# VectorE takes two low parts of the second attention earlier, and one of them from GpSimd

## The chip, the core and the metric

The program runs on one core of one Trainium2 chip. The metric is the device time of one execution in microseconds (us); lower is better. The engines of the core are named as the profile names them: PE is TensorE's matmul (PEld its weight loads), DVE is VectorE, ACT is ScalarE, POOL is GpSimd, SP is SyncE, which here only issues DMAs. Each engine runs its own list of instructions in the order in which it was written, and waits on semaphores for the others.

## What is computed

Two transformer layers on 4 batches of 512 tokens of width 256. The first layer is a softmax attention and a linear layer, the second a lightning attention with 16 heads of width 128 and a mixture of 8 experts. In each layer both halves stand between a normalisation with a modulation per batch and a gated addition to the residual `x`:

```python
h = _layernorm(x, axis=-1) * (1 + ca) + sa
x = x + ga * _L0_attn_ref(h, ...)
h = _layernorm(x, axis=-1) * (1 + cb) + sb
x = x + gb * _L0_ffn_ref(h, ...)
...
h = _layernorm(x, axis=-1) * (1 + ca) + sa
x = x + ga * _L1_attn_ref(h, ...)     # the second attention
h = _layernorm(x, axis=-1) * (1 + cb) + sb
x = x + gb * _L1_ffn_ref(h, ...)
```

The second attention, cut to what it multiplies (silu is applied to q, k and v, and the decays depend on the head):

```python
qkv = jax.nn.silu(jnp.einsum('bnf,of->bno', x, w_qkv))
o_inter = jnp.einsum('bhmd,bhde->bhme', qi * q_decay, kv)
qk = jnp.einsum('bhmd,bhnd->bhmn', qi, ki) * diag_decay
o_intra = jnp.einsum('bhmn,bhne->bhme', qk, vi)
out = norm_w * (out * jax.lax.rsqrt(var + EPS))
gate = jax.nn.sigmoid(jnp.einsum('bnf,of->bno', x, w_gate))
return jnp.einsum('bno,fo->bnf', gate * out, w_out)
```

## The kernel before

The work is written by hand as one list per engine. Before the second attention stands the front stage (the first layer), behind it the experts stage. `attention1_stage` is the second attention. It runs over 8 pairs of heads (`PAIRS`), and within a pair over 8 units (`UNITS`): a unit is one batch and one head of the pair, 512 tokens. `attention1_order` gives PE's order within a unit `u`: four blocks of scores `("s", u, 0..3)`, the projections `k` and `q` of the next unit, two projections `v` (or the output product `y`), the projection `g` of the gate, and the four products `pv` of the unit before. Scores and projections share a ring of four PSUM banks; PE waits for a bank until the engine that reads it is through (`emptied`).

**High and low parts.** Products in single precision are made of three products of fp32r parts. ACT copies a tensor into its high part, and a subtraction (whole minus high) makes the low part: `low` in DVE's list, line 1727, or `lower` of `LastPost`, line 372. PE can take a tensor only when its low part is there. `silu_split` on ACT makes the silu of q or k (line 1619) and its high part (line 1622), and `qk_low(which, unit, it)` on DVE the low part, where `which` is 1 for k and 0 for q. The first unit's k and q carry the number -1, and are projected before the second attention begins. `masked` (line 1746) is DVE's product of a block of scores in PSUM and the decay mask; `scores_hi` (line 1647) and `scores_low` (line 1727, tile `attn_pp`) split it. The scores of unit 0 wait for `qk_low(1, -1, 0)` and `qk_low(0, -1, 0)` (`k_ready`, `q_ready`).

**The first layer's last batch.** The front stage leaves the last of the four batches unfinished; `LastPost` ends it inside the first pair of the second attention, spread over the units:

- `tensor_at`, `scalar_aot`, `tensor_out` (lines 264, 271, 278 and 280): the attention's output product, ahead of everything else of the stage.
- `vector_attended` (lines 286 and 295) gates it and adds it to `x`; `vector_stats` (lines 317 and 320) takes mean and variance; `pool_rstd` (lines 327 to 334) takes the reciprocal root.
- `scalar_norm` (line 341), on ACT at the end of unit 0, normalises; `tensor_turn` (line 350), on PE in unit 1 ahead of `("s", 1, 1)`, transposes; `scalar_ht` (lines 362 and 367), on ACT in unit 1, modulates and makes the high part; `lower` (line 372) the low part, before the change on POOL.
- `tensor_ff` (line 380), on PE ahead of `("k", 2)`, is the linear layer, 24 matmuls. It waits for `low_done`, which `lower` raises. A second round of norm, turn, `scalar_ht` and `lower` follows in units 3 and 4 for the second attention's own input of that batch; its `lower` is on DVE already.

POOL also makes the low parts of the first pair's weights, in three parts (line 1873: 1280, 512 and 256 columns), and sums squares (line 1883). SP clears the table of expert rows in DRAM and loads the next pair's weights.

Of the kernel before, what the change touches and what calls it, by code (L numbers as in the profile page):

```python
# [1304 lines left out]
def attention1_stage(nc, t, d):  # L1305
# [14 lines left out]
    with ExitStack() as ctx:  # L1320
# [26 lines left out]
        post = LastPost(n, t, ps, Y_BANK, late_norm.ht)  # L1347
# [60 lines left out]
        with nc.Block() as block:  # L1408
# [316 lines left out]
            def _(dve):  # L1725
# [55 lines left out]
                dve.wait_ge(norm_loaded, 16)  # L1781
                nc.vector.tensor_scalar(normw[:, :], normw[:, :], 0.5, None, ALU.mult).then_inc(norm_halved, 1)
                dve.wait_ge(norm_halved, 1)
                post.vector_attended(nc, dve)
                post.vector_stats(nc, dve, 0)
                qk_low(1, -1, 0)
                qk_low(0, -1, 0)

                def body(it, first, last_pair):
                    for u in range(UNITS):  # L1790
                        more = not (last_pair and u == UNITS - 1)
                        if u == 2:

                            dve.wait_ge(wo_loaded, it * 16 + 16)
                            for h in range(2):
                                nc.vector.tensor_scalar(woraw[:, h, :], woraw[:, h, :], normw[:, at(it * 2 + h)], None,
                                                        ALU.mult).then_inc(wo_scaled, 1)
                        if late(it, u, 2):
                            gate_unit(u - 2, it)
                        masked(u, 0, it)  # L1800
                        if late(it, u, 2):
                            y_low(u - 2, it)
                        if first and u == 3:
                            post.vector_stats(nc, dve, 1)
                        scores_low(u, 0, it)
                        masked(u, 1, it)
                        if more:
                            qk_low(1, u, it)
                        scores_low(u, 1, it)
                        if u == UNITS - 2 and not last_pair:  # L1810
                            weights_low(0, it + 1)
                        if u == UNITS - 1 and not last_pair:
                            weights_low(1, it + 1)
                        if u == 0 and not first:
                            weights_low(2, it)
                        masked(u, 2, it)
                        if first and u == 2:
                            post.vector_fed(nc, dve)
                        if last_pair and u == NORM_AT:
                            late_norm.vector_mean(nc, dve, 0, 0, Y_BANK)  # L1820
                        if last_pair and u == NEXT_AT:
                            late_norm.vector_mean(nc, dve, 1, 1, Y_BANK)
                        if last_pair and u == TURN_AT - 1:
                            late_norm.vector_stats(nc, dve, 0, 0)
                        if last_pair and u == TURN_AT:
                            late_norm.vector_norm(nc, dve, 0, 0)
                        if more:
                            qk_low(0, u, it)
                        scores_low(u, 2, it)
                        if first and u == 4:  # L1830
                            post.lower(dve, nc.vector, 1)
                        masked(u, 3, it)
                        if u % 2 == 0:
                            values_low(0, u, it)
                        elif late(it, u, 3):
                            if not first and u == 1:
                                dve.wait_ge(zeroed, 1)
                            if last_pair and u == UNITS - 1:
                                gate_unit(u - 1, it)
                            else:  # L1840
                                add_output(u, 0, it, first)
                        scores_low(u, 3, it)
                        if u % 2 == 0:
                            values_low(1, u, it)
                        elif late(it, u, 3) and not (last_pair and u == UNITS - 1):
                            add_output(u, 1, it, first)
# [15 lines left out]
            @block.gpsimd  # L1862
            def _(pool):
                nc.gpsimd.memset(t["ones1"][:, :], 1.0).then_inc(ones_set, 1)
                nc.gpsimd.memset(empty[:, 0:D], 0.0).then_inc(empty_set, 1)
                nc.gpsimd.memset(empty[:, D:D + 2], -1.0).then_inc(empty_set, 1)
                nc.gpsimd.memset(empty[:, D + 2:D + 4], 0.0).then_inc(empty_set, 1)
                nc.gpsimd.iota(no_token[:, :], [[P, E * B * TB]], base=2 * B * S, channel_multiplier=1,
                               allow_small_or_imprecise_dtypes=True).then_inc(empty_set, 1)

                def weights_low(part, it):
                    pool.wait_ge(w_hi[part], it + 1)
                    nc.gpsimd.tensor_tensor(wp[:, 1, :, PART[part]], wraw[:, :, PART[part]],
                                            wp[:, 0, :, PART[part]].bitcast(F32), ALU.subtract).then_inc(w_ready[part], 1)

                def sum_unit(u, it):

                    b, h = (u % UNITS) // 2, u % 2
                    pool.wait_ge(squared, it * UNITS + (u + 1))
                    if h == 1:  # L1880
                        pool.wait_ge(summed, it * UNITS + u)
                    cols = ssq[:, b * S:(b + 1) * S]
                    nc.gpsimd.tensor_tensor(cols, cols, sq[:, h, :], ALU.add).then_inc(summed, 1)  # L1883

                sums_zeroed = n.sem("sums_zeroed")
                for b in (0, 2):
                    nc.gpsimd.memset(ssq[:, b * S:(b + 1) * S], 0.0).then_inc(sums_zeroed, 1)
                for part in (1, 0, 2):
                    weights_low(part, 0)
                post.pool_rstd(nc, pool, 0)  # L1890

                def body(it, first, last_pair):
                    for u in range(UNITS):
                        if first and u == 1:
                            nc.gpsimd.memset(yacc[:, NT - TB:NT, :], 0.0).then_inc(zeroed, 1)
                            nc.gpsimd.memset(ssq[:, S:2 * S], 0.0).then_inc(sums_zeroed, 1)
                            post.pool_biased(nc, pool)
                            post.lower(pool, nc.gpsimd, 0)
                        if first and u == 3:
                            post.pool_rstd(nc, pool, 1)  # L1900
                            nc.gpsimd.memset(ssq[:, 3 * S:4 * S], 0.0).then_inc(sums_zeroed, 1)
                            pool.wait_ge(sums_zeroed, 4)
                        if late(it, u, 2):
                            if first and u == 2:
                                pool.wait_ge(sums_zeroed, 3)
                            sum_unit(u - 2, it)
                        if first and u == 2:
                            post.pool_fed(nc, pool)
                        if u == 2:
                            pool.wait_ge(wo_hi, it + 1)  # L1910
                            nc.gpsimd.tensor_tensor(wop[:, 1], woraw[:, :, :], wop[:, 0].bitcast(F32),
                                                    ALU.subtract).then_inc(wo_ready, 1)
                        if last_pair and u == NORM_AT:
                            late_norm.pool_rms(nc, pool, 0, 0)
                            late_norm.pool_update(nc, pool, 0, 0)
                        if last_pair and u == TURN_AT - 1:
                            late_norm.pool_rstd(nc, pool, 0)
                        if last_pair and u == NEXT_AT:
                            late_norm.pool_rms(nc, pool, 1, 1)
                        if last_pair and u == NEXT_AT + 1:  # L1920
                            late_norm.pool_update(nc, pool, 1, 1)

                over_pairs(pool, body)
                for u in (UNITS - 2, UNITS - 1):
                    sum_unit(u, PAIRS - 1)
                late_norm.pool_rstd(nc, pool, 1)
# [1092 lines left out]
```

## Time and profile before

| | us |
|---|---|
| median of three runs | 1178.83 |
| lowest, highest | 1176.25, 1179.16 |
| the profiled execution | 1185.24 |
| its span, first to last instruction | 1183.4 |
| PE busy in it | 1069.6 (90%) |
| DVE busy | 918.9 (78%) |
| ACT busy | 734.4 (62%) |
| POOL busy | 337.7 (29%) |
| mean granted TensorE clock | 0.953 of full |

The second attention begins in the trace 262 us after the span's start and ends at about 975 us. From 330 to 975 us PE is busy for 641.78 of 645 us. Times in the rows below count from the span's start. A row of the timeline gives an instruction's start and how long it took, or the first start and the whole time of several merged ones. Two instructions of one engine may overlap by about 0.1 us, since an engine starts one that doesn't depend on the one before while that drains. A wait names the engine whose signal came last.

### The profile page before, as it was taken

What the parts mean: (1) busy time and instruction counts of PE and PEld (TensorE: products, weight loads), DVE (VectorE), ACT (ScalarE), POOL (GpSimd) and SP (SyncE); (2) the same over time, 40 slices, a digit from 0 to 9 for tenths busy, and PEclk for the clock granted to TensorE, in tenths of its full rate; (3) what the DMA queues carried; (4) which work ended last, traced back from release to release, by engine and by line L of the source; (5) the groups of instructions that cost most, each with busy time, mean ns of one, the idle gap of its engine ahead of it and who ended that gap; (6) DMA issues with size and microseconds to landing.
All of it is one profiled execution on the core that took longest, in us unless ns stands there. A gap on an engine that the chain in (4) does not pass through costs nothing. (4 is left out here: it accounts for less than half of the span.)

```text
span 1183.4 us, 21636 instructions
## 1 busy us (share of the span) xinstructions
PE 1069.6 (90%) x7268; PEld 917.4 (78%) x7268; DVE 918.9 (78%) x1859; ACT 734.4 (62%) x1390; POOL 337.7 (29%) x347
## 2 busy tenths in 40 slices
PE   6879787777999999999999999999999997769994
PEld 5645555556888998899889988998999886659992
DVE  6688888846778878788778778788788788777775
ACT  5668686766567566666666666666666654625650
POOL 3375454443311111101111111111111244743440
PEclk9989898978999999999999999999999998879997
DMA  7210000109504004004004003004001000453436
GB/s 276 71 45 10 15 6 15 41 22 81 118 1 126 10 2 125 9 9 116 9 9 116 9 9 116 9 9 116 9 13 33 1 1 27 141 175 100 127 91 222
DMA packets 62326, 72.16 MB, mean 61 GB/s; under 512 B 21842, under 2 KB 49618, under 8 KB 61235
## 3 DMA queue, kind: packets, MB, share of 16 engines
q1 hardware_dynamic: 58850, 61.90, 19.9%
q0 software_dynamic: 3408, 9.39, 2.1%
q8 instruction: 39, 0.64, 0.2%
q14 instruction: 29, 0.23, 0.1%
HBM read 36.39 MB, written 32.78 MB: 58 GB/s over the span
## 5 line engine op out<-in xcount | busy, mean ns | idle before, releaser
L1475 PE MATMUL all_psum<-all_h_parts,attn_wp 128*128 128x512 f32 x1140 | 296.7, 396 | 0.0
L1647 ACT CAST attn_pp<-attn_p 128x512 fp32r<-128x512 f32 (+3 forms) x256 | 117.4, 458 | 200.8 <-DVE attn_p L1746 198.7
L1475 PEld LDWEIGHTS all_psum<-all_h_parts,attn_wp 128*128 128x128 f32 x1140 | 209.4, 189 | 39.6
L1883 POOL TENSOR_TENSOR all_gate<-all_gate,attn_sq 128x512 f32<-128x512 f32 x64 | 84.8, 1325 | 496.3 <-ACT attn_sq L1658 496.2
L1727 DVE TENSOR_TENSOR attn_pp<-attn_p,attn_pp 128x512 fp32r<-128x512 f32 (+3 forms) x256 | 200.1, 782 | 8.6 <-ACT attn_pp L1647 8.6
L1554 PE MATMUL all_psum<-attn_qkp 128*128 128x512 f32 (+3 forms) x768 | 164.6, 323 | 7.7 <-DVE attn_qkp L1727 7.7
L1501 PE MATMUL all_psum<-attn_pp,attn_vp 128*128 128x512 f32 (+3 forms) x768 | 163.2, 321 | 1.1 <-DVE attn_pp L1727 0.6
L1501 PEld LDWEIGHTS all_psum<-attn_pp,attn_vp 128*128 128x128 f32 x768 | 128.9, 189 | 21.6 <-issue 1.4
L1554 PEld LDWEIGHTS all_psum<-attn_qkp 128*128 128x128 f32 x768 | 124.4, 190 | 16.4 <-DVE attn_qkp L1727 6.2
L1746 DVE TENSOR_TENSOR attn_p<-all_psum,attn_mask 128x512 f32<-128x512 f32 (+3 forms) x256 | 123.7, 483 | 6.6 <-PE all_psum L1554 5.4
L1003 DVE TENSOR_REDUCE front_top<-all_psum 128x2 f32<-128x256 f32 (+3 forms) x128 | 100.8, 816 | 26.5 <-PE all_psum L650 26.2
L1727 DVE TENSOR_TENSOR attn_yp<-attn_y,attn_yp 128x512 fp32r<-128x512 f32 x64 | 45.6, 713 | 77.2 <-ACT attn_yp L1655 77.2
L803 ACT ACTIVATE front_probs<-all_psum 128x1024 f16<-128x1024 f32 (+3 forms) x128 | 83.4, 707 | 33.8 <-PE all_psum L657 33.7
L1470 PE MATMUL all_psum<-attn_wp,all_h_parts 128*128 128x256 f32 x768 | 100.6, 280 | 0.0
L1485 PE MATMUL all_psum<-all_wop,attn_yp 128*128 128x256 f32 x744 | 96.5, 278 | 0.8 <-DVE attn_yp L1727 0.8
L1727 DVE TENSOR_TENSOR attn_qkp<-attn_qk,attn_qkp 128x512 fp32r<-128x512 f32 x128 | 88.1, 689 | 10.2 <-ACT attn_qkp L1622 10.2
L1470 PEld LDWEIGHTS all_psum<-attn_wp,all_h_parts 128*128 128x128 f32 x768 | 94.6, 188 | 0.0
L1485 PEld LDWEIGHTS all_psum<-all_wop,attn_yp 128*128 128x128 f32 x744 | 91.0, 188 | 1.0 <-DVE attn_yp L1727 1.0
L1622 ACT CAST attn_qkp<-attn_qk 128x512 fp32r<-128x512 f32 x128 | 79.5, 621 | 4.1
L1619 ACT ACTIVATE attn_qk<-all_psum 128x512 f32<-128x512 f32 x128 | 75.7, 592 | 3.4 <-PE all_psum L1475 3.3
L657 PE MATMUL all_psum<-front_qt,front_kt 128*128 128x512 f16 (+3 forms) x256 | 56.5, 333 | 19.2 <-ACT front_probs L803 8.7
L1727 DVE TENSOR_TENSOR attn_vp<-attn_v,attn_vp 128x512 fp32r<-128x512 f32 x64 | 44.3, 692 | 32.1 <-ACT attn_vp L1640 32.1
(375 smaller groups left out, 1844.6 us busy)
## 6 DMA issues: line engine op xcount, KB each, us to landing
expert_rows<-attn_empty SPq DMA_DIRECT2D x8, 2080.0 KB, 11.3
all_wraw<-in_w1p SPq DMA_DIRECT2D x8, 1024.0 KB, 5.9
all_yacc<-expert_rows SPq DMA_DIRECT2D x39, 130.5 KB
attn_mask<-decay_masks SPq DMA_DIRECT2D x16, 256.0 KB, 2.7
experts_wx<-expert_results SPq DMA_DIRECT2D x6, 512.0 KB, 8.3
experts_xraw<-in_wx SPq DMA_DIRECT2D x4, 608.0 KB
all_wraw<-in_wx SPq DMA_DIRECT2D x4, 608.0 KB
all_x<-in_x SPq DMA_DIRECT2D x4, 512.0 KB, 7.3
```

Source lines behind the costliest of these rows:

```text
L803: nc.scalar.activation(probs[:, pr, j, :, 0:S - j * P], banks(ev)[:, :, 0:S - j * P], ACT.Exp, scale=D0 ** -0.5).then_inc(exp_done, 1)
L1003: nc.vector.tensor_reduce(top[:, tt, h:h + 2], banks(ev)[:, :, 0:(tt + 1) * P], AX.X, ALU.max).then_inc(top_done, 1)
L1470: last = nc.tensor.matmul(out[:, i * 2 * P:(i + 1) * 2 * P], hh[:, a, k, tt * P:(tt + 1) * P], wp[:, c, k, col:col + 2 * P], start=(m == 0 ...
L1475: last = nc.tensor.matmul(out, wp[:, a, k, col:col + P], hh[:, c, k, b * S:(b + 1) * S], start=(m == 0), stop=(m == 5))
L1485: last = nc.tensor.matmul(ps[:, Y_BANK + i, half * D:(half + 1) * D], yp[:, a, h, tt * P:(tt + 1) * P], wop[:, c, h, :], start=(m == 0), s ...
L1501: last = nc.tensor.matmul(ps[:, O_BANK + h, j * P:S], vp[:, b % 2, a, j, h * P:(h + 1) * P], pp[:, h, c, OFF[j]:OFF[j] + S - j * P], start ...
L1554: last = nc.tensor.matmul(bank(task)[:, 0:S - j * P], qkp[:, h, a, 1, j * P:(j + 1) * P], qkp[:, h, c, 0, j * P:S], start=(m3 == 0), stop= ...
L1622: nc.scalar.copy(qkp[:, (unit + 1) % 2, 0, which, :], qk[:, which, :]).then_inc(hi_sem, 1)
L1647: nc.scalar.copy(pp[:, u % 2, 0, cols], p[:, cols]).then_inc(p_hi, 1)
L1727: nc.vector.tensor_tensor(out, whole, high.bitcast(F32), ALU.subtract).then_inc(ready, 1)
L1746: nc.vector.tensor_tensor(p[:, cols], bank(task)[:, 0:S - j * P], mask[:, u % 2, 0:S - j * P], ALU.mult).then_inc(p_masked, 1)
L1883: nc.gpsimd.tensor_tensor(cols, cols, sq[:, h, :], ALU.add).then_inc(summed, 1)
```

## The change

Two edits, both in `attention1_stage`. The low parts of the first unit's k and q are issued on DVE ahead of `vector_attended` and `vector_stats` instead of behind them. And the first `lower` of `LastPost` goes from POOL's list in unit 1 to DVE's list in unit 1, between `qk_low(0, 1, 0)` and `scores_low(1, 2, 0)`. No instruction is added or dropped.

```diff
@@ DVE's list, ahead of the first pair
                 dve.wait_ge(norm_halved, 1)
+                qk_low(1, -1, 0)
+                qk_low(0, -1, 0)
                 post.vector_attended(nc, dve)
                 post.vector_stats(nc, dve, 0)
-                qk_low(1, -1, 0)
-                qk_low(0, -1, 0)
@@ DVE's list, within a unit
                         if more:
                             qk_low(0, u, it)
+                        if first and u == 1:
+                            post.lower(dve, nc.vector, 0)
                         scores_low(u, 2, it)
@@ POOL's list, within a unit
                             post.pool_biased(nc, pool)
-                            post.lower(pool, nc.gpsimd, 0)
                         if first and u == 3:
```

DVE's list at the start of the second attention, as a difference. `attn_qkp` holds the parts of q and k, `attn_post_st` and `attn_post_mv` the statistics of the last batch:

```order
 L1782 TENSOR_SCALAR attn_normw<-attn_normw 128x16
+L1727 TENSOR_TENSOR attn_qkp<-attn_qk,attn_qkp 128x512 x2
 L286 TENSOR_TENSOR all_yacc<-all_psum,all_gate 128x1024
 L295 TENSOR_TENSOR all_x<-all_x,all_yacc 128x1024
 L317 BN_STATS attn_post_st<-all_x 128x6 x4
 L320 BN_AGGR attn_post_mv<-attn_post_st 128x2 x4
-L1727 TENSOR_TENSOR attn_qkp<-attn_qk,attn_qkp 128x512 x2
```

The two subtractions moved past ten instructions; the next instruction after the statistics is now the first `masked` of unit 0 (line 1746).

DVE's list in the middle of unit 1, after the change. `attn_p` and `attn_pp` are the masked scores and their parts, `attn_n_ht` the modulated transpose of the last batch, `all_h_parts` the parts of the layer's input:

```order
268 L1746 TENSOR_TENSOR attn_p<-all_psum,attn_mask 128x256
269 L1727 TENSOR_TENSOR attn_qkp<-attn_qk,attn_qkp 128x512
270 L372 TENSOR_TENSOR all_h_parts<-attn_n_ht,all_h_parts 128x2x512
271 L1727 TENSOR_TENSOR attn_pp<-attn_p,attn_pp 128x256
272 L1746 TENSOR_TENSOR attn_p<-all_psum,attn_mask 128x128
```

Line 372 is new there; before, the row of 128x256 scores followed the q part directly.

POOL's list around the instruction that left it, before the change. `attn_sq` holds a unit's squares, which go into the sums in `all_gate`:

```order
151 L1896 MEMSET all_gate 128x512
152 L303 TENSOR_TENSOR all_x<-all_x,all_gate 128x1024
153 L372 TENSOR_TENSOR all_h_parts<-attn_n_ht,all_h_parts 128x2x512
154 L1883 TENSOR_TENSOR all_gate<-all_gate,attn_sq 128x512
155 L310 TENSOR_TENSOR all_x<-all_x,all_yacc 128x1024
```

After it, line 303 is followed by the sum of squares.

## Rows read from the trace of the kernel before

**Rows 1.** Waits of PE, 250 to 345 us: total, times, longest.
```profile
PE all_psum L1554 <- DVE attn_qkp L1727: 5.8, 1, 5.8
...
PE all_psum L380 <- POOL all_h_parts L372: 3.1, 1, 3.1
PE all_psum L350 <- DVE all_yacc L1777: 1.3, 1, 1.3
```

**Rows 2.** Timeline of PE: start, us, instruction, idle before and its releaser.
```profile
266.92 0.63 PE L280 MATMUL all_psum<-all_yacc 128*128 128x256 f16 x2
273.33 1.62 PE L1554 MATMUL all_psum<-attn_qkp 128*128 128x512 f32 x3 [5.78 <-DVE attn_qkp L1727]
...
279.26 0.52 PE L1554 MATMUL all_psum<-attn_qkp 128*128 128x256 f32 x3
...
282.76 1.55 PE L1475 MATMUL all_psum<-all_h_parts,attn_wp 128*128 128x512 f32 x6
...
293.05 0.91 PE L1554 MATMUL all_psum<-attn_qkp 128*128 128x512 f32 x3
297.10 4.61 PE L380 MATMUL all_psum<-all_wop,all_h_parts 128*128 128x256 f32 x24 [3.13 <-POOL all_h_parts L372]
...
306.42 1.57 PE L1470 MATMUL all_psum<-attn_wp,all_h_parts 128*128 128x256 f32 x12
```

**Rows 3.** Timeline of DVE.
```profile
267.67 1.23 DVE L286 TENSOR_TENSOR all_yacc<-all_psum,all_gate 128x1024 f32<-128x1024 f32 x1 [0.63 <-PE all_psum L280]
268.93 1.23 DVE L295 TENSOR_TENSOR all_x<-all_x,all_yacc 128x1024 f32<-128x1024 f32 x1
...
271.92 1.26 DVE L1727 TENSOR_TENSOR attn_qkp<-attn_qk,attn_qkp 128x512 fp32r<-128x512 f32 x2
274.99 0.69 DVE L1746 TENSOR_TENSOR attn_p<-all_psum,attn_mask 128x512 f32<-128x512 f32 x1 [1.80 <-PE all_psum L1554]
...
294.87 2.36 DVE L1727 TENSOR_TENSOR attn_pp<-attn_p,attn_pp 128x256 fp32r<-128x256 f32 x1 [2.03 <-ACT attn_pp L1647]
...
334.87 1.22 DVE L372 TENSOR_TENSOR all_h_parts<-attn_n_ht,all_h_parts 128x1024 fp32r<-128x1024 f32 x1
```

**Rows 4.** Timeline of ACT.
```profile
267.84 0.62 ACT L1622 CAST attn_qkp<-attn_qk 128x512 fp32r<-128x512 f32 x1
...
275.71 0.62 ACT L1647 CAST attn_pp<-attn_p 128x512 fp32r<-128x512 f32 x1 [6.43 <-DVE attn_p L1746]
...
284.85 2.06 ACT L341 ACTIVATE all_yacc<-all_x,attn_post_shift,attn_post_rstd 128x256 f32<-128x256 f32 x4
...
293.49 1.05 ACT L367 CAST all_h_parts<-attn_n_ht 128x1024 fp32r<-128x1024 f32 x1
294.44 0.40 ACT L1647 CAST attn_pp<-attn_p 128x256 fp32r<-128x256 f32 x1
```

**Rows 5.** Timeline of POOL.
```profile
274.42 0.20 POOL L334 TENSOR_TENSOR attn_post_shift<-attn_post_shift,attn_post_rstd 128x4 f32<-128x4 f32 x1
...
294.61 2.34 POOL L372 TENSOR_TENSOR all_h_parts<-attn_n_ht,all_h_parts 128x1024 fp32r<-128x1024 f32 x1 [5.21 <-ACT all_h_parts L367]
```

**Rows 6.** POOL by form, 255 to 345 us: busy us, mean ns, idle before.
```profile
L1873 POOL TENSOR_TENSOR attn_wp<-all_wraw,attn_wp 128x512 fp32r<-128x512 f32 x1 | 2.2, 2231 | 2.1 <-ACT attn_wp L1611 2.1
L1911 POOL TENSOR_TENSOR all_wop<-attn_woraw,all_wop 128x512 fp32r<-128x512 f32 x1 | 1.3, 1290 | 3.1 <-ACT all_wop L1710 3.1
...
L1873 POOL TENSOR_TENSOR attn_wp<-all_wraw,attn_wp 128x256 fp32r<-128x256 f32 x1 | 0.7, 722 | 0.0
```

**Rows 7.** Busy us by stretch, granted clock, DMA share, GB/s.
```profile
273.33:277.40 4.07, 4.07 (x10) 3.20 (x11) 1.38 (x2) 0.62 (x1) 2.49 (x4) 0.50 0.97 25
...
275.71:284.35 8.64, 8.64 (x51) 7.72 (x50) 4.97 (x11) 6.42 (x12) 0.26 (x1) 0.90 0.71 3
297.90:301.30 3.40, 3.40 (x19) 3.40 (x18) 2.14 (x6) 1.76 (x4) 0.00 (x0) 0.50 1.09 220
320.00:340.00 20.00, 18.15 (x108) 15.63 (x108) 14.52 (x26) 14.61 (x29) 4.63 (x5) 1.00 0.00 1
```

The columns of rows 7 after the stretch and its length are PE, PEld, DVE, ACT and POOL, each with its instructions in brackets.

## The prediction

> **What bounds the kernel now.** The table of busy times comes first: PE is busy for 1069.6 of 1183.4 us, and between 330 and 975 us for all but 3 of 645 us. In that long stretch only PE's own work counts, and the change adds and removes none there. So the change can pay only where PE stands still ahead of it, in the first units of the second attention; what PE wins there arrives at 330 us undiminished, because behind it PE waits for almost nothing. I therefore read PE's waits from 250 to 345 us next. Two of them are the two places of the change: 5.8 us for the low parts of the first unit's q and k (line 1554 behind line 1727), and 3.1 us for the low part on POOL (line 380 behind line 372); a third, 1.3 us for DVE at line 350, comes later and is not touched [rows 1]. Then the timelines of the engines around these two places, to see what would be late next. The reader is to see in them that at the first place PE, DVE and ACT hand work to one another within a few tenths of a us, so that PE's wait is not simply the gain.
>
> **First edit, on PE.** PE ends the output product at 267.55 and starts the first scores at 273.33 [rows 2]. It waits for two subtractions on DVE that start at 271.92 and end at 273.18 [rows 3]; PE follows 0.15 later. They stand behind the gated addition and the statistics. Their own input is there much earlier: ACT ends q's high part at 267.84 + 0.62 = 268.46 [rows 4], and k's before that. DVE is free from 267.67 - 0.63 = 267.04 on [rows 3]. Issued first, k's low part runs in the wait for q's, and q's starts 0.04 after ACT's end, at 268.50, and lasts half of 1.26 and a little, 0.69: until 269.19. PE starts at 269.34 instead of 273.33, 3.99 us earlier. That is the upper bound of this edit.
>
> **First edit, on DVE.** The work that was first is now behind. Line 286 starts at about 269.1 instead of 267.67, and so does what follows: the addition (line 295) at 269.1 + 1.26 = 270.36 where it was at 268.93. From its start to the end of the statistics DVE took 271.92 - 268.93 = 2.99 [rows 3]. So the first `masked` can start at 270.36 + 2.99 = 273.35, where it started at 274.99. It no longer waits for PE but for DVE's own list. Its gain is 1.64 us, not 3.99.
>
> **A collision on the way.** POOL makes weights' low parts at this time. Its 512 columns took 2.23 us beside the addition, and another subtraction of 512 columns 1.29; the next part, 256 columns, 0.72 [rows 6]. So the two engines hold each other off: POOL lost 0.94 us while DVE's addition ran. The reverse is in the trace too: DVE's line 1727 of 294.87 took 2.36 us and ended at 297.23, just behind POOL's line 372, which ended at 296.95 [rows 3, 5]. In the new order q's low part runs first, POOL's 512 columns from about 269.1 to 270.4, and then DVE's addition and POOL's 256 columns want to start within 0.1 us. If DVE gets there first it loses 0.1 us, if POOL does 0.1 + 0.72 = 0.8. The first `masked` starts between 273.4 and 274.2, a gain of 0.8 to 1.6 us.
>
> The Trainium skill, SBUF — State Buffer, section Who interferes with whom and the section before it on the two sides, says that VectorE and GpSimd share one pair of ports under an exclusive lock, held for a whole instruction by whichever starts first, where VectorE's instruction has two inputs in SBUF. It speaks against this edit, since the addition now meets POOL's parts. By it alone the sum would have the 0.1 or the 0.8 us above and nothing between; the rows of line 372 agree, with 2.36 us.
>
> **First edit, on ACT.** What PE needs next comes through ACT, which has the high parts of all scores, the silus, and at the end of unit 0 the normalisation of the last batch (line 341). From its first high part at 275.71 to the gate at 284.35 ACT was busy for 6.42 of 8.64 us [rows 4, 7]; the other 2.22 us are waits, mostly for PE's projections, 4 us earlier now. ACT starts 0.8 to 1.6 us earlier and can lose those 2.2 us: the normalisation comes 3.0 to 3.8 us earlier than at 284.85. PE's own bound is the gate's projection (282.76, 1.55 us), 4.0 us earlier. PE's third block of scores, at 279.26 before and at 275.3 now, needs the first `masked` to be through, at 274.1 to 274.9: just no wait. The transpose (line 350) waits for ACT's normalisation, not for PE, and stays with ACT: **3.4 us**, the middle, since the two ends of the collision differ by 0.1 us in timing and no row decides between them. The statistics end 1.4 to 2.2 us later; POOL's root behind them ended at 274.62 [rows 5], ten us ahead of the normalisation. That delay costs nothing while more than 5 us of that slack are left.
>
> From the normalisation to the high part of its transpose (ends at 293.49 + 1.05 = 294.54 [rows 4]) everything follows on ACT, POOL's line 303 and DVE in a fixed pattern, so the whole pattern moves by 3.4 us.
>
> **Second edit.** After the scores of unit 2 PE stands from 293.97 until 297.10 [rows 2]. ACT hands over at 294.54; POOL takes 2.34 us, from 294.61 to 296.95, and PE follows at 297.10. The same subtraction on DVE takes 1.22 us in unit 4 [rows 3]. DVE is idle then: it waits 2.03 us for ACT's high part of the scores, which ends at 294.84, after the one that the new instruction needs. So 294.61 + 1.22 + 0.15 = 295.98: **1.1 us**. The instruction that it pushes back, the low part of 256 scores columns, ended at 297.23 because of POOL; now it starts at 295.8 and ends well before that. POOL is rid of 2.34 us, and had waited 5.21 us for that instruction's input [rows 5]; nothing else hangs on it there. Cover gone would cost 1.22 us of DVE; here the cover is DVE's own wait.
>
> **The clock.** PE ran at half clock from 297.90 to 301.30, so the granted clock fell after the idle 3.13 us [rows 7]. The 24 matmuls of line 380 took 4.61 us; 12 of the same width at full clock took 1.57, so 24 take 3.1, and the fall cost 1.5 us [rows 2]. Shortened to about 2.0 us the idle time lies between this one and the 1.3 us ahead of line 350, in a stretch whose clock stayed at 1.00 [rows 1, 7]. It is nearer to the shorter one, but not by enough to book: bounds 0 and 1.5 us, and I take 0. At the start PE worked at half clock until 277.40, for 4.07 us after it had begun [rows 7]. I expect about the same length again; a longer one is a rival below.
>
> **The sum.** 3.4 + 1.1 = 4.5 us. The profiled execution, 1185.24 us with a span of 1183.4, would take 1180.7; it stands 6.4 us above the median, by work that the change doesn't touch, so I take the 4.5 us off the median: 1178.8 - 4.5 = **1174.3 us**. The terms alone leave 4.1 to 4.9, so 1173.9 to 1174.7, and the three runs of before differ by 2.9 us, so 1172.8 to 1175.8 is this case's own range.
>
> **Rivals.**
>
> - *The clock stays up at line 380.* Forecast and another 1.5 us: 1172.8. For it speaks the idle time of 1.3 us without a fall; against it that the only other length seen here, 3.13, fell.
> - *DVE and ACT pace unit 0.* The hand-overs between DVE and ACT keep their rhythm, and PE waits for them where it didn't before. Then only the first `masked`'s 0.8 to 1.6 us arrive: 1.2 + 1.1 = 2.3 us, 1176.5. For it: the third block of scores has only 0.4 to 1.2 us of room, and ACT in order puts the first block's high part ahead of k's silu. Against it: ACT's 2.22 us of waits.
> - *It gives nothing.* The start is hidden by something that I don't see, such as the mask's or the weights' DMAs, which fill the DMA engines at that time (share 0.97 [rows 7]), or the win is given back in the experts stage, behind 975 us: 1178.8. DVE's wait for PE ahead of the first `masked` shows that the mask was there at 274.99, not that it was at 273.4.
> - *Slower: the half clock lasts.* PE starts 4 us earlier into work that DVE feeds later, at 273.4 to 274.2. If it stops for it and the clock therefore stays at half through unit 0 and into unit 1, up to the end of the normalisation, then what PE did at full clock from 277.40 to 284.85 + 2.06 = 286.91 takes 9.5 us more: 4.0 - 9.5 + 1.1 = -4.4, so 1183.2. It decides against the change from the point where about 5 us of full-clock work fall to half, that is if the clock comes up 9 us after PE's start and not 4.
>
> **How the numbers follow.** A measurement of this kernel can tell about 0.3%, 3.5 us, from no change: faster means below 1175.3. Forecast 0.45, of which four fifths lie below that; clock stays up 0.20; paced by DVE and ACT 0.20, nearly all within; nothing 0.09; slower 0.06. Faster is 0.36 + 0.19 + 0.02 = 0.57, slower 0.05, the rest, 0.38, within. The range reaches from the clock's rival with the runs' spread, 1171.9, over the forecast and the paced case to 1177.6; outside remain most of the last two cases and a little at the lower end.
>
> **What would show it.** Right: PE's wait ahead of the first scores is 1.8 us and not 5.8; DVE's first `masked` starts 4.1 to 4.9 us after those scores began and waits for nothing; line 341 starts about 3.4 us earlier, at 281.4; line 372 appears on DVE with 1.2 us, and PE's wait ahead of line 380 is 2.0. POOL's parts of 512 and 256 columns or line 295 show a duration longer than 1.3, 0.7 or 1.2, and which of them tells who lost the collision. The granted clock after line 380's start tells the first rival. Wrong: PE waits at line 1475 or 1554 within unit 0, line 341 moves by less than 3 us, or unit 0 has half clock beyond 6 us. If both waits shrink as written and the time doesn't, it was given back behind 975 us.

## The result

The changed kernel is faster: 1172.0 us median (20 runs, 1168.7 to 1176.3) against 1178.5 us of the kernel before (20 runs, 1173.6 to 1182.2 but for one of 1236.8), ratio 0.9947 with a 95% interval of 0.9932 to 0.9961. That is 6.2 us less, between 4.6 and 8.0; the ratio leaves out the run of 1236.8 us as a slow one, which is why it gives 6.2 and not the 6.5 between the two medians. The forecast was 1174.3 us, within 1171.9 to 1177.6: the median lies only 0.1 us above the lower end.

Two profiled executions can't be compared by their spans alone: 1183.4 us before and 1168.4 after are 15 us apart, more than twice what the runs show. So I count from a fixed event ahead of the change, PE's first transposes of the stage (line 264; 262.62 us before, 262.15 after). The place farther on at which I read the sum is the first output product behind 350 us (line 1485, in unit 7, the last of the first pair): 363.73 us before and 356.99 after, that is 101.11 and 94.84 us behind the transposes. **6.27 us are won by then**, as much as the 6.2 us measured. What more the two spans differ by (15 us less 6.27) arises elsewhere: 0.5 us ahead of the transposes, and most of the rest behind the second attention, where the logits (line 1602) start at 988.70 and 982.09, 6.14 us apart counted in the same way.

PE's waits in the changed kernel, 250 to 345 us (total, times, longest), at the places of [rows 1]:

```profile
...
PE all_psum L380 <- DVE all_h_parts L372: 2.0, 1, 2.0
PE all_psum L1554 <- DVE attn_qkp L1727: 1.8, 1, 1.8
PE all_psum L350 <- DVE all_yacc L1777: 1.4, 1, 1.4
...
```

Against [rows 1] the wait ahead of the first scores fell from 5.8 to 1.8, the one ahead of line 380 from 3.1 to 2.0, and its releaser is DVE instead of POOL. PE's timeline, the lines that answer to [rows 2]:

```profile
262.15 1.01 PE L264 MATMUL all_psum<-all_ident,all_yacc 128*128 128x128 f16 x8 [3.93 <-PEq L2920]
...
268.87 1.62 PE L1554 MATMUL all_psum<-attn_qkp 128*128 128x512 f32 x3 [1.78 <-DVE attn_qkp L1727]
...
273.45 1.54 PE L1475 MATMUL all_psum<-all_h_parts,attn_wp 128*128 128x512 f32 x6
...
278.53 1.57 PE L1475 MATMUL all_psum<-all_h_parts,attn_wp 128*128 128x512 f32 x6
...
291.91 3.06 PE L380 MATMUL all_psum<-all_wop,all_h_parts 128*128 128x256 f32 x24 [1.96 <-DVE all_h_parts L372]
...
356.99 1.53 PE L1485 MATMUL all_psum<-all_wop,attn_yp 128*128 128x256 f32 x12
```

Line 380 takes 3.06 us and not 4.61. The granted clock over these matmuls (third number from the right, columns as in [rows 7]), before and after:

```profile
297.10:301.71 4.61, 4.61 (x25) 4.61 (x26) 2.98 (x9) 2.43 (x5) 0.02 (x1) 0.63 1.10 210
291.91:294.97 3.06, 3.06 (x25) 3.06 (x26) 2.41 (x7) 1.00 (x3) 0.00 (x0) 1.00 1.17 8
```

1.00 is full clock, 2.4 GHz; before, most of the stretch ran at half of it, 1.2 GHz. DVE's timeline, for [rows 3]:

```profile
268.03 0.69 DVE L1727 TENSOR_TENSOR attn_qkp<-attn_qk,attn_qkp 128x512 fp32r<-128x512 f32 x1 [0.38 <-ACT attn_qkp L1622]
268.64 1.22 DVE L286 TENSOR_TENSOR all_yacc<-all_psum,all_gate 128x1024 f32<-128x1024 f32 x1
269.89 1.76 DVE L295 TENSOR_TENSOR all_x<-all_x,all_yacc 128x1024 f32<-128x1024 f32 x1
...
273.43 0.66 DVE L1746 TENSOR_TENSOR attn_p<-all_psum,attn_mask 128x512 f32<-128x512 f32 x1
...
290.54 1.23 DVE L372 TENSOR_TENSOR all_h_parts<-attn_n_ht,all_h_parts 128x1024 fp32r<-128x1024 f32 x1 [1.74 <-ACT all_h_parts L367]
291.68 0.42 DVE L1727 TENSOR_TENSOR attn_pp<-attn_p,attn_pp 128x256 fp32r<-128x256 f32 x1
```

The addition (line 295) took 1.76 us where it took 1.23; the first masked block starts without a wait, in DVE's own order; the low part of the 256 columns takes 0.42 us where [rows 3] have 2.36. ACT's timeline, for [rows 4], with the gate of unit 0 and the normalisation:

```profile
274.12 0.62 ACT L1647 CAST attn_pp<-attn_p 128x512 fp32r<-128x512 f32 x1 [5.30 <-DVE attn_p L1746]
...
280.34 0.59 ACT L1629 ACTIVATE attn_gate<-all_psum 128x512 f32<-128x512 f32 x1
280.83 2.06 ACT L341 ACTIVATE all_yacc<-all_x,attn_post_shift,attn_post_rstd 128x256 f32<-128x256 f32 x4
```

And ACT's load in between, by stretch (columns as in [rows 7]):

```profile
274.12:280.34 6.22, 6.22 (x42) 5.60 (x41) 4.77 (x10) 6.02 (x12) 2.61 (x5) 1.00 1.24 19
```

From its first high part to the gate ACT has 6.02 us of work in 6.22 us; before it was 6.42 in 8.64 ([rows 7]). The 6.27 us divide by these rows, all counted from the transposes: line 341 comes 22.23 - 18.68 = 3.55 us earlier; line 380 34.48 - 29.76 = 4.72, so 1.17 more; and its 24 matmuls take 4.61 - 3.06 = 1.55 us less.

### The profile page after: what moved, and what is told of

Same layout as the page of the kernel before. It is cut to its first block and busy times, and to the rows that moved or that the text cites. A ratio compares the mean times of both kernels' runs of the same rounds, so it can differ in the third digit from the quotient of the medians.

```text
span 1168.4 us, 21636 instructions
## 1 busy us (share of the span) xinstructions
PE 1062.5 (91%) x7268; PEld 909.7 (78%) x7268; DVE 919.3 (79%) x1860; ACT 734.3 (63%) x1390; POOL 334.3 (29%) x346
```

## The experiments

The theory is that these three terms are what the change brings: one for each edit and one for the clock, the last because the second edit made the wait ahead of line 380 shorter. The rivals: that the clock behind this wait was chance or came with the first edit's shift, and, for each edit, that another engine was late anyway. Eleven kernels were run; "transposes" below is the start of line 264 in the same profile.

| kernel | ratio to before, 95% interval | wait ahead of L380 | L380 takes | L341 behind transposes | L380 | unit 7's output |
|---|---|---|---|---|---|---|
| before | 1 | 3.13 | 4.61 | 22.23 | 34.48 | 101.11 |
| changed | 0.9947 (0.9932 to 0.9961) | 1.96 | 3.06 | 18.68 | 29.76 | 94.84 |
| first edit only | 0.9975 (0.9957 to 0.9993) | 3.10 | 4.60 | 18.67 | 30.92 | 97.54 |
| second edit only | 0.9977 (0.9958 to 0.9997) | 1.97 | 3.08 | 21.98 | 33.07 | 98.15 |
| low part twice | 0.9971 (0.9949 to 0.9992) | 3.23 | 4.60 | 18.67 | 31.02 | 97.65 |
| low part and half | one run | 2.68 | 4.60 | 18.68 | 30.48 | 97.13 |
| no collision | one run | 1.97 | 3.12 | 18.22 | 29.30 | 94.46 |
| statistics later | 0.9944 (0.9926 to 0.9961) | 1.98 | 3.08 | 18.31 | 29.40 | 94.51 |
| and k first | 0.9936 (0.9912 to 0.9959) | 1.96 | 3.06 | 17.78 | 28.86 | 93.95 |
| linear layer later | 0.9939 (0.9914 to 0.9963) | 0.58 | 3.09 | 18.67 | 29.77 | 94.29 |
| all three moves | 0.9926 (0.9901 to 0.9952) | 0.56 | 3.07 | 17.78 | 28.86 | 93.40 |
| bias add later | 0.9948 (0.9931 to 0.9965) | 1.13 | 3.12 | 18.68 | 28.93 | 95.01 |
| five moves | 0.9938 (0.9917 to 0.9959) | none | 3.01 | 17.72 | 28.08 | 94.06 |

All columns but the ratio are us of one profile each. What the change doesn't touch repeats from kernel to kernel within some hundredths of a us counted from the transposes, so a column tells differences of a tenth, where the timed runs leave several us open. Each ratio is to the kernel before timed beside it; the changed kernel was not timed beside the others, so a variant and the changed kernel are compared only through their two ratios.

### Each edit alone

The first edit, as a difference to the kernel before:

```diff
+                qk_low(1, -1, 0)
+                qk_low(0, -1, 0)
                 post.vector_attended(nc, dve)
                 post.vector_stats(nc, dve, 0)
-                qk_low(1, -1, 0)
-                qk_low(0, -1, 0)
```

> The first edit alone: the low parts of the first unit's k and q ahead of the gated addition and the statistics; the last batch's low part stays on POOL. Theory (each edit pays by itself, and the clock pays only where the wait ahead of line 380 is shortened): PE's wait ahead of the first scores 1.8 us, the normalisation at line 341 comes 3.5 us earlier counted from PE's first transposes, the wait ahead of line 380 stays 3.1 us and the granted clock falls behind it; 3.5 us less than before, ratio 0.9970. Rival (the first edit shifted PE's work so that the clock stayed up, and the length of the wait has nothing to do with it): 24 matmuls of line 380 in 3.1 us behind a wait of 3.1 us; 5.0 us less, ratio 0.9957.

The wait ahead of line 380 stayed, and the clock fell behind it:

```profile
295.11 4.60 PE L380 MATMUL all_psum<-all_wop,all_h_parts 128*128 128x256 f32 x24 [3.10 <-POOL all_h_parts L372]
```

At unit 7's output 3.57 us are won, and 2.9 us (0.8 to 5.1) in the times. The rival with 5.0 us is out by the profile: the shift alone didn't keep the clock up in it.

The second edit:

```diff
+                        if first and u == 1:
+                            post.lower(dve, nc.vector, 0)
                         scores_low(u, 2, it)
...
-                            post.lower(pool, nc.gpsimd, 0)
```

> The second edit alone: the last batch's low part on DVE; the first unit's low parts stay behind the statistics. Theory: PE's wait ahead of the first scores stays 5.8 us, the wait ahead of line 380 is 2.0 us, and the clock stays up mostly: 1.2 + 1.5 = 2.7 us less than before, ratio 0.9977. Rival (the clock behind that wait is chance and no part of the change's gain): 1.2 us less, ratio 0.9990, and line 380's 24 matmuls in 4.6 us.

```profile
294.55 3.08 PE L380 MATMUL all_psum<-all_wop,all_h_parts 128*128 128x256 f32 x24 [1.97 <-DVE all_h_parts L372]
```

2.96 us won at unit 7's output, of which 0.25 in unit 0 (line 341 at 21.98 instead of 22.23), where the granted clock rose a little sooner in this execution; the other 2.7 are 1.16 us of the wait and 1.53 of the clock. The times give 2.7 us (0.4 to 5.0), so the readings of 2.7 and 1.2 us are told apart by the profile and not by the times. The two edits' gains, 3.57 and 2.7, make 6.27: they add up.

### The length of the wait and the clock

The extra subtraction, as a difference to the changed kernel, like those of all runs that follow:

```diff
                         if first and u == 1:
+                            dve.wait_ge(post.high_done, 1)
+                            nc.vector.tensor_tensor(hh[:, 1, :, (B - 1) * S:B * S], post.ht[:, :, :],
+                                                    hh[:, 0, :, (B - 1) * S:B * S].bitcast(F32), ALU.subtract
+                                                    ).then_inc(post.lowered_once, 1)
+                            dve.wait_ge(post.lowered_once, 1)
                             post.lower(dve, nc.vector, 0)
```

> The changed kernel with the last batch's low part made twice in a row on DVE, the second one releasing PE. It doubles the cost that the second edit cut: PE's wait ahead of line 380 becomes 2.0 + 1.3 = 3.3 us. Theory (a wait of this length lets the clock fall): 1.3 + 1.5 = 2.8 us more than the changed kernel, so 3.5 us less than before, ratio 0.9970, line 380's matmuls in 4.6 us. Rival (clock by chance): 1.3 us more than the changed kernel, 4.9 us less than before, ratio 0.9958.

```profile
PE all_psum L380 <- DVE all_h_parts L372: 3.2, 1, 3.2
```

The matmuls took 4.60 us. Unit 7's output came 97.65 - 94.84 = 2.81 us later than in the changed kernel: 1.26 for the second subtraction and 1.54 for the clock, as expected. In the times it stands at 3.4 us less than before where the theory had 3.5 and the rival 4.9; the interval, 0.9 to 6.0, holds both. So the verdict rests on the profile. The same with half the columns in the extra subtraction:

> The changed kernel with half of the last batch's low part (512 of 1024 columns) made once more on DVE ahead of the whole. PE's wait ahead of line 380 becomes 2.0 + 0.65 = 2.6 us, between the lengths at which the clock stayed up (2.0, five profiles of five) and fell (3.1 to 3.2, three of three). Theory (the length decides, and the limit lies somewhere between): line 380's matmuls take either 3.1 or 4.6 us, which narrows the limit. Rival (a gradual loss): between, about 3.8 us.

```profile
291.43 4.60 PE L380 MATMUL all_psum<-all_wop,all_h_parts 128*128 128x256 f32 x24 [2.68 <-DVE all_h_parts L372]
```

2.68 us let it fall, in full and not by a part. Taken together: behind idle times of 2.0 us or less line 380 took 3.01 to 3.12 us in all nine profiles with such a wait or none, five of them with 1.96 to 1.98 us; behind 2.68, 3.10, 3.13 and 3.23 us it took 4.60 or 4.61, four of four. That is one profile of each of the thirteen kernels in the table.

It doesn't follow that 2.0 us is safe. Late in the last pair every one of these kernels has a further wait of 1.95 or 1.96 us, at a place that no move touches, with PE at work at full clock ahead of it. The kernel before and the changed kernel:

```profile
954.39 0.93 PE L1554 MATMUL all_psum<-attn_qkp 128*128 128x512 f32 x3 [1.95 <-DVE attn_qkp L1727]
955.16 1.56 PE L1475 MATMUL all_psum<-all_h_parts,attn_wp 128*128 128x512 f32 x6
```

```profile
947.65 0.94 PE L1554 MATMUL all_psum<-attn_qkp 128*128 128x512 f32 x3 [1.96 <-DVE attn_qkp L1727]
948.42 2.39 PE L1475 MATMUL all_psum<-all_h_parts,attn_wp 128*128 128x512 f32 x6
```

In the kernel before the granted clock over the 5 us behind this wait was 1.00, in the changed kernel 0.66. It fell there in four profiles of thirteen (changed, second edit only, no collision, bias add later) and stayed at 1.00 in the other nine. So of 18 waits of 1.95 to 1.98 us 14 kept the clock and 4 lost it, and the four of 2.68 us and more ahead of line 380 all lost it. A shorter wait makes the fall less likely and doesn't rule it out. What else decides stays open, and so does how often line 380 meets a fall in the timed runs, which have no granted clock for a stretch.

### The collision of line 295

```diff
-                for part in (1, 0, 2):
+                for part in (1, 0):
                     weights_low(part, 0)
                 post.pool_rstd(nc, pool, 0)
+                weights_low(2, 0)
```

> The changed kernel with POOL's weights' part of 256 columns behind the root of the variance instead of ahead of the statistics, so that it can't meet DVE's addition (line 295), which took 1.76 us and not 1.23. Theory (the addition lost 0.5 us to that part, and the loss goes through DVE and ACT to the normalisation): line 295 takes 1.2 us, and line 341 starts 0.5 us earlier, 18.2 us behind PE's first transposes where it was 18.7. Rival (PE hides it): line 295 is shorter, line 341 stays at 18.7 us. Times can't tell 0.5 us, the profile can.

```profile
268.57 1.23 DVE L295 TENSOR_TENSOR all_x<-all_x,all_yacc 128x1024 f32<-128x1024 f32 x1
...
279.05 2.07 ACT L341 ACTIVATE all_yacc<-all_x,attn_post_shift,attn_post_rstd 128x256 f32<-128x256 f32 x4
```

With the transposes at 260.83 the normalisation is 18.22 us behind them, 0.46 earlier than in the changed kernel, and the first masked block 0.54 earlier. So DVE's and ACT's delays in unit 0 reach the normalisation nearly in full, and POOL's 256 columns cost the change 0.46 us there and 0.38 us at unit 7's output.

### What is late next in unit 0

```diff
                 post.vector_attended(nc, dve)
-                post.vector_stats(nc, dve, 0)
...
                         masked(u, 0, it)
+                        if first and u == 0:
+                            post.vector_stats(nc, dve, 0)
```

> The changed kernel with the statistics of the last batch behind the first masked block instead of ahead of it. DVE reaches the first masked block 1.8 us earlier. Theory (with that, PE's own work up to the gate's projection is what ends last, and it ended at 280.1 where the gate began at 280.34): the normalisation at line 341 comes only 0.2 us earlier, 18.5 instead of 18.7 us behind PE's first transposes; ratio to before 0.9945, within noise of the changed kernel. Rival (ACT and DVE alone pace unit 0): 1.8 us earlier, 16.9 us behind the transposes, ratio 0.9932.

Line 341 came 18.31 us behind the transposes, 0.37 us earlier: nearer to 0.2 than to 1.8. PE has no more to give there: its projection for the gate (278.46, 1.55 us) ends at 280.01, and ACT takes it at 280.06. Then PE, too, was let ahead:

```diff
-                    for task in order:
+                    for task in ([("k", 0), ("s", 0, 0)] + order[2:] if first else order):
```

> As the one before, and PE makes the projection of k for unit 1 ahead of the scores of unit 0, in the wait of 1.8 us that is left. Theory: PE and DVE are both 1.8 us earlier, so the normalisation is 1.6 to 1.8 us earlier than in the changed kernel, 17.0 us behind the transposes; ratio to before 0.9932. Rival (the half clock lasts longer because PE has begun earlier, and takes it back): less than 1 us earlier. The wait ahead of line 380 stays 2.0 us; its matmuls take 3.1 us if the length of the wait decides on the clock.

A miss: 17.78 us, 0.90 earlier than in the changed kernel and not 1.6 to 1.8. The rival's figure came out (less than 1 us) but not its cause: the granted clock was 1.00 from 273.2 us on, 3.4 us after this kernel's PE had begun. PE waited for ACT's silus, and ACT for DVE:

```profile
276.49 1.67 PE L1470 MATMUL all_psum<-attn_wp,all_h_parts 128*128 128x256 f32 x12 [0.53 <-ACT attn_qk L1619]
...
279.15 1.70 PE L1470 MATMUL all_psum<-attn_wp,all_h_parts 128*128 128x256 f32 x12 [0.49 <-ACT attn_qk L1619]
```

```profile
276.47 0.62 ACT L1622 CAST attn_qkp<-attn_qk 128x512 fp32r<-128x512 f32 x1
278.09 0.51 ACT L1647 CAST attn_pp<-attn_p 128x384 fp32r<-128x384 f32 x1 [1.00 <-DVE attn_p L1746]
```

The statistics, moved from in front of the first masked block, stood in front of the second: counted from the transposes the first came 1.83 us earlier than in the changed kernel (9.45 instead of 11.28), the second only 0.89 (12.34 instead of 13.23).

### The wait ahead of line 380, and what lies behind it

```diff
-                        if first and task == ("k", 2):
+                        if first and task == ("pv", 2, 0):
                             pe.wait_ge(post.ht_done, 1)
                             post.tensor_ff(nc, pe)
```

> The changed kernel with the 24 matmuls of the last batch's linear layer one task later on PE: behind the projection of k in unit 2 instead of ahead of it, so that this projection (1.55 us) runs in the wait of 2.0 us. Theory (PE's wait ahead of line 380 counts in full): the wait shrinks to 0.4 to 0.5 us, 1.5 us less than the changed kernel, 7.7 us less than before, ratio 0.9935; no half clock there in any profile. Rival (DVE and ACT pace units 2 and 3, and PE waits later instead): no gain over the changed kernel, ratio 0.9947, with a new wait of about 1.5 us in unit 2 or 3.

The wait shrank from 1.96 to 0.58 us as expected, but at unit 7's output only 94.84 - 94.29 = 0.55 us were left of it. The rival has the rest. At the second block of scores of unit 2 PE is 1.35 us ahead of the changed kernel; then it meets DVE, which takes 2.62 us instead of 0.42 beside POOL's addition of line 310 at the end of unit 2. The changed kernel has the same collision (2.63 us), but there PE came later and didn't wait. DVE began that instruction 39.25 us behind the transposes where it was 39.79: it was only 0.54 us ahead before it, just what is left at unit 7's output. It had waited 0.37 and 0.46 us for PE's scores in the changed kernel, could win no more than that, and lost some of it on the next low part of `attn_qkp` beside POOL's sum of squares (1.32 us instead of 0.86). DVE's, POOL's and PE's timelines of this kernel:

```profile
301.72 2.62 DVE L1727 TENSOR_TENSOR attn_pp<-attn_p,attn_pp 128x256 fp32r<-128x256 f32 x1
...
306.06 0.69 DVE L1727 TENSOR_TENSOR attn_vp<-attn_v,attn_vp 128x512 fp32r<-128x512 f32 x1 [0.72 <-ACT attn_vp L1640]
```

```profile
301.28 2.77 POOL L310 TENSOR_TENSOR all_x<-all_x,all_yacc 128x1024 f32<-128x1024 f32 x1 [2.56 <-DVE all_yacc L286]
```

```profile
306.85 0.92 PE L1501 MATMUL all_psum<-attn_pp,attn_vp 128*128 128x512 f32 x3 [0.58 <-issue]
```

The profile names no releaser for PE's wait (`issue`); it ended 0.10 us behind the low part of v on DVE (306.06 + 0.69 = 306.75).

> The two moves before and the linear layer one task later together. Theory (the gains lie at different places of one chain and add up): 1.7 + 1.5 = 3.2 us less than the changed kernel, 9.4 us less than before, ratio 0.9920. Rival (behind unit 2 DVE and ACT pace the work, and what PE wins first is lost to them): not below the linear layer's move alone, ratio 0.9939.

94.84 - 93.40 = 1.44 us less than the changed kernel at unit 7's output, the sum of 0.89 and 0.55, and not the 3.2 expected. In the times 8.7 us less than before (5.7 to 11.7), the lowest ratio of all kernels; against the changed kernel's 6.2 the difference is no larger than the intervals.

### A collision between the normalisation and line 380

```diff
     def pool_biased(self, nc, pool):
-        pool.wait_ge(self.xn_done, 1)
+        pool.wait_ge(self.low_done, 1)
```

> The changed kernel with POOL's addition of the bias term to x (line 303) waiting for the last batch's low part instead of the normalisation, so that it runs behind line 372 and no longer beside DVE's low part of unit 1's first scores, which took 2.47 us instead of 0.69. Theory (that collision lies on the chain from the normalisation to line 380: ACT waits 1.86 us for the next masked block): DVE's instruction takes 0.7 us, the next masked block starts when PE has made it, 1.3 us earlier, and line 380 comes 1.3 us earlier, 28.5 us behind PE's first transposes where it was 29.8; ratio to before 0.9936. Rival (the chain waits for PE's turn and projections in any case): line 380 at 29.8 us, ratio 0.9947.

The instruction took 0.69 us, and line 380 came 0.83 us earlier, two thirds of what was expected, since DVE now waited for PE's scores (0.47 and 0.57 us). But POOL's line 303, moved behind line 372, met the next low part there:

```profile
291.34 1.84 DVE L1727 TENSOR_TENSOR attn_pp<-attn_p,attn_pp 128x128 fp32r<-128x128 f32 x1 [0.37 <-ACT attn_pp L1647]
```

It took 1.84 us where it took 0.29, and unit 7's output came 0.17 us later than in the changed kernel. DVE came to this instruction 0.84 us ahead of the changed kernel (29.68 us behind the transposes against 30.52) and began the next one 0.72 us behind it (31.45 against 30.73). The gain was handed back there; no run took this collision away by itself.

> The three moves of the run of that name, POOL's 256 columns behind the root, and the bias term's addition later. Theory (the gains on the chain to line 380 add up): line 380 0.5 to 1.8 us earlier than with the three moves, where it stood 28.9 us behind the first transposes, PE's wait ahead of it gone; 1.5 us less than with the three moves, ratio to before 0.9913. Rival (DVE's collision with POOL's line 310 in unit 2 takes back what PE wins, as it took 0.8 of 1.35 us from the linear layer's move): no gain over the three moves, 0.9926.

Line 380 stands 28.08 us behind the transposes, 0.78 earlier than with three moves, and has no wait. At unit 7's output it is 94.06, 0.66 us later than with three. The rival was right that it gives nothing more, and the times agree (0.9938), but the collision was another than the rival's: it is the one of the run before, beside line 303. DVE came to it 0.89 us ahead of the three moves (28.73 us behind the transposes against 29.62) and left it 0.66 behind (30.49 against 29.83), the same 0.66 as at unit 7's output. The collision with line 310 was there with three moves too, 2.62 us then and 2.60 now.

## Why the prediction was right, and where it was not

The time lies in the range, the waits and their order came as written, and the clock's term did not. That the median is inside, by 0.1 us, is owed to the lower end, which was drawn by the clock's rival; the forecast's own terms with the runs' spread gave 1172.8 to 1175.8, and the median lies below that.

**First edit, on PE.** Right to a hundredth: 10.71 - 6.72 = 3.99 us earlier, with a wait of 1.78 us left.

**On DVE and the collision.** The first masked block started 4.56 us after the scores had begun, within 4.1 to 4.9. The collision happened, and DVE lost 0.53 us in it, between the two ends of 0.1 and 0.8: POOL's 512 columns took their plain 1.29 us this time, its 256 columns their plain 0.7, and DVE paid:

```profile
268.59 1.98 POOL L1875 TENSOR_TENSOR attn_wp<-all_wraw,attn_wp 128x512 fp32r<-128x512 f32 x2 [2.03 <-ACT attn_wp L1611]
```

and by form:

```profile
L1875 POOL TENSOR_TENSOR attn_wp<-all_wraw,attn_wp 128x512 fp32r<-128x512 f32 x1 | 1.3, 1288 | 2.0 <-ACT attn_wp L1611 2.0
```

POOL was the first, which in the prediction was the case of 0.8 us. Its two parts ended at 270.57, and the addition at 271.65, that is 1.08 us later and not its plain 1.23. The run without the collision shows what it cost.

**On ACT.** Right: ACT's waits went, 0.20 us are left of 2.22, and the normalisation came 3.55 us earlier (forecast 3.4, bounds 3.0 and 3.8). The rival of DVE and ACT keeping their pace is refuted by that. That ACT's start then set the normalisation is shown by the run without the collision: the first masked block 0.54 us earlier gave 0.46. That PE is right behind is shown by the statistics' move: DVE 1.8 us earlier gave 0.37.

**The statistics' delay.** Costless as said; POOL's root behind them ended at 275.53 us, 5.3 us ahead of the normalisation.

**Second edit.** Right: 1.23 us on DVE, a wait of 1.96 us, 1.17 us won (forecast 1.1).

**The clock: the term that was mis-sized.** The step weighed the idle time of 2.0 us between 1.3 (clock stays) and 3.13 (clock falls), called it nearer to the shorter, and booked 0 of a possible 1.5 us. It was 1.55. The first rival, with 0.20, was what happened: forecast 4.5 and measured 6.27 differ by 1.55 for the clock, 0.15 for the first edit and 0.07 for the second. The five profiles with waits of about 2.0 us ahead of line 380 show no fall, so the term belonged in the sum; the last pair's waits of the same length, with four falls in thirteen, show that it was not certain, and that all of it came in this profile was partly luck. By those 14 of 18 an estimate of the term is 1.2 us (14/18 of 1.55). The prediction said that the only other length seen was 3.13 us. That was an oversight: it looked at waits up to 345 us, and the same trace has the wait of 1.95 us at 954.39, with a granted clock of 1.00 behind it.

**The other rivals.** What PE won arrived undiminished in the last pair: its wait at 954.39 and 947.65 ends 691.77 and 685.50 us behind the transposes, 6.27 apart. The fall of the clock there then cost the changed kernel's profile 1.5 us, and by the logits the two are 6.14 apart again; where it had them back is open. Nothing was given back behind the second attention that the runs could show. The slower one fell at the start: PE ran through unit 0 without a wait, and its second projection, 4.6 us behind its start, took the 1.54 us of full clock already (the row of 273.45 above); the granted clock was 0.50 until 273.0, for 4.1 us as before. And the mask was there in time: the first masked block (273.43) waited for nothing. The rival "the clock stays up at line 380" is the one that came true.

## What to carry to other kernels

A wait at which an idle time ends is worth more than its length if the clock would have fallen behind it: cutting 1.2 us from one wait saved 2.7 in the profile. Book the clock's part with a chance and not as certain, and look for waits of the new length in the whole trace, not only near the change. Before a step is moved ahead, look at what it now stands in front of on its own engine and at whom that feeds; here the chain went over to DVE and ACT after 3.55 of 3.99 us, and further moves in the same unit brought tenths. And a subtraction or addition with both inputs in SBUF on DVE should not meet one on POOL: moving POOL's instruction only helps if its new place is free too.

## What the runs showed of the hardware

At line 380, with PE busy at full clock ahead of the wait, the clock fell behind idle times of 2.68 us and more (four of four) and stayed up behind 1.98 us and less (nine of nine). Behind the last pair's wait of 1.95 or 1.96 us, also with PE busy at full clock ahead, it fell in four profiles of thirteen. In the changed kernel it also fell behind a wait of 0.77 us at 248.33 us; there PE had been busy for only 2.13 us between 244 and 248 us, at a granted clock of 1.00. Where it fell at line 380, 24 matmuls of 256 columns took 4.6 us instead of 3.06, always by the same 1.54 to 1.55 us.

DVE and POOL hold each other off by whole instructions. DVE's 128 columns took 1.84 us instead of 0.29, its 256 columns 2.62 instead of 0.42 and its 512 columns 2.47 instead of 0.69, each beside one POOL addition of 1024 columns. This is what the Trainium skill, SBUF — State Buffer, section Who interferes with whom, says of the port pair that the two engines share, and the traces agree. It also says that the order of issue decides who is blocked. In the changed kernel POOL's second part began 0.05 us ahead of DVE's addition, and the addition paid; with that part moved away it took its 1.23 us again. In these rows DVE's instruction ended its plain time less 0.14 or 0.15 us behind POOL's: 0.28 for 256 columns, 0.55 for 512, 1.08 for 1024.
